# Zeros for the routed rows in two parts, another column order, ranks and slot table earlier in the last step

## What is computed

```
x = x + _layernorm(_L0_attn_ref(_layernorm(x), ...))
xf = _layernorm(x).reshape(-1, C)
shared = geglu(xf, w1s, w2s, w3s)
idx = jnp.argmax(xf @ Wg, axis=-1)
for e in range(N_EXPERTS):
    y = geglu(xf, W1[e], W2[e], W3[e])      # (256, 1024), (256, 1024), (1024, 256)
    final = final + jnp.where((idx == e)[:, None], y, 0.0)
x = x + _layernorm(shared + final)
```

## Time and profile before

| | us |
|---|---|
| median of 3 runs | 1071.74 (1070.04 to 1072.08) |
| the profiled execution's own time | 1071.29 |
| its span in the trace | 1069.4 |
| PE busy in the span | 932.4 (87%) |
| DVE, ACT, POOL busy | 770.1, 599.7, 592.8 |

### The profile page before, as it was taken

The page is one execution under the profiler, slowest core; times in us unless marked ns, Lnnn a source line. Parts: engine busy times, 40 slices in busy tenths (PEclk is TensorE's granted clock), DMA queues, the critical chain, the costliest instruction groups (busy, mean ns, idle before and its releaser), DMA issues.

```text
span 1069.4 us, 28305 instructions
## 1 busy us (share of the span) xinstructions
PE 932.4 (87%) x9798; PEld 830.3 (78%) x9798; DVE 770.1 (72%) x1680; ACT 599.7 (56%) x1031; POOL 592.8 (55%) x802
## 2 busy tenths in 40 slices
PE   2285999999999899899899898845999999999994
PEld 2264787887787787788787787645999999999994
DVE  6889999999999999999999974531444444444443
ACT  5386687688688688678678665312333333333331
POOL 5435477577477577577578523222545455555553
PEclk9687999999999999999999998887999999999998
DMA  6120441441441341341343323298577886585620
GB/s 234 51 89 10 138 159 43 139 159 40 137 157 42 135 157 50 127 157 55 132 147 119 119 80 119 108 371 286 187 236 244 272 275 221 191 262 179 207 66 21
DMA packets 84130, 158.35 MB, mean 148 GB/s; under 512 B 5421, under 2 KB 62894, under 8 KB 78960
## 3 DMA queue, kind: packets, MB, share of 16 engines
q1 hardware_dynamic: 32560, 74.87, 19.9%
q10 hardware_dynamic: 46960, 65.85, 19.0%
q0 software_dynamic: 4560, 16.98, 4.1%
HBM read 178.31 MB, written 52.64 MB: 216 GB/s over the span
## 4 chain that ended last, share of the span: by engine, by line
PE 28%; DVE 26%; issue 14%; POOL 9%; ACTq 5%; ACT 3%; DMA 2%; SPq 2%; DVEq 0%; POOLq 0%
PE up L318 6%; PE up L319 6%; PE up L320 6%; DVE mixed L952 3%; PE yp L320 2%; PE yp L319 2%; PE yp L318 2%; DVE er L1022 2%; ACTq L828 2%; DVE gu L1149 2%; DVE arena L927 2%; POOL inv L1403 2%; DVE val L1037 2%; POOL sh_s L1484 2%; DVE state L1001 2%
## 5 line engine op out<-in xcount | busy, mean ns | idle before, releaser
L318 PE MATMUL up<-mix_s,arena 128*128 128x128 f16 x1248 | 212.1, 220 | 0.9 <-DVE mix_s L1351 0.5
L319 PE MATMUL up<-mix_s,arena 128*128 128x128 f16 x1248 | 212.1, 220 | 0.0
L320 PE MATMUL up<-mix_s,arena 128*128 128x128 f16 x1248 | 212.0, 220 | 0.0
L1484 POOL TENSOR_TENSOR sh_s<-gu,sh_s 128x512 f16<-128x512 f32 x64 | 81.9, 1281 | 169.4 <-ACT sh_s L731 169.3
L318 PE MATMUL up<-xf_s,arena 128*128 128x256 f16 x512 | 142.3, 278 | 0.0
L320 PE MATMUL up<-xf_s,arena 128*128 128x256 f16 x512 | 142.2, 278 | 0.0
L319 PE MATMUL up<-xf_s,arena 128*128 128x256 f16 x512 | 142.2, 278 | 0.0
L1575 POOL TENSOR_TENSOR kf_s<-ex,kf_s 128x512 f16<-128x512 f32 x78 | 90.3, 1157 | 86.2 <-ACT kf_s L889 86.1
L1356 DVE SCALAR_TENSOR_TENSOR ex<-up,ex 128x512 f32<-128x512 f32 x78 | 54.0, 692 | 103.7 <-ACT ex L883 103.6
L318 PEld LDWEIGHTS up<-mix_s,arena 128*128 128x128 f16 x1248 | 122.5, 98 | 2.4 <-DVE ex L1356 1.1
L319 PEld LDWEIGHTS up<-mix_s,arena 128*128 128x128 f16 x1248 | 122.5, 98 | 0.4
(11 more groups left out here) (234 smaller groups left out, 2976.7 us busy)
## 6 DMA issues: line engine op xcount, KB each, us to landing
arena<-w_split ACTq DMA_DIRECT2D x117, 1024.0 KB
arena<-in_W SPq DMA_DIRECT2D x24, 1024.0 KB, 8.1
w_split<-arena SPq DMA_DIRECT2D x24, 1024.0 KB, 8.3
rows<-routed_rows ACTq DMA_DIRECT2D x39, 260.0 KB
routed_rows<-ex SPq DMA_DIRECT2D x8, 1170.0 KB, 12.9
normed<-routed_rows ACTq DMA_DIRECT2D x39, 128.0 KB
x_in<-in_x SPq DMA_DIRECT2D x16, 256.0 KB, 2.8
x_res<-in_x SPq DMA_DIRECT2D x16, 256.0 KB, 2.7
```

The costliest lines, as they stand in the source:

```text
L318: pe.matmul(out, stat(0), mov(0), start=first, stop=False)
L319: pe.matmul(out, stat(0), mov(1), start=False, stop=False)
L320: return pe.matmul(out, stat(1), mov(0), start=False, stop=last)
L1484: pool.tensor_tensor(sh_s[:, 1, 2 * g:2 * g + 2, :], gu[g % GUS][:], sh_s[:, 0, 2 * g:2 * g + 2, :], ALU.subtract).then_inc(S("sh_lo"), 1)
```

## The change

The records' columns are put in another order: the shared part first, then X1, then ID, OFF and XF, so that ID, OFF and XF are one part of 260 floats. The zeros are written in two parts. The first writes columns ID and up only, over five blocks of 128 rows for each expert, at the end of step 15 (when chunk 13 is placed), from a cleared piece of `x_in`; the scatter of chunk 14 waits for it. The second writes the first 520 columns of one block of 128 rows for each expert, in step 17, behind the last placing. In step 17 the ranks, the placing and the slot table are computed next to the gate's choice, woven into the first two shared products; the scatter of the part with XF comes first on POOL; the split of (7, 2) on DVE moves from step 17 to the end of step 16; and ACT loads slot 1's weights after it has copied the shared output (`second_slot`).

```diff
-XF, SHARED, X1, ID, OFF = 0, PART, PART + C, PART + 2 * C, PART + 2 * C + 1
+SHARED, X1, ID, OFF, XF = 0, PART, 2 * PART, 2 * PART + 1, 2 * PART + 4
-        zero_row = ex.rearrange("p n k c -> p (n k c)")[:, 0:ROW]
+        zero_row = x_in.rearrange("p t d -> p (t d)")[:, 0:ROW - ID]
+        zero_rest = ex.rearrange("p n k c -> p (n k c)")[:, 2 * CT * CH:2 * CT * CH + ID]
# SP
-                n = CH // P + 1
+                n = 2 * CH // P + 1
...
-                    sp.dma_start(routed_rows[bass.ds(at, n * P)].rearrange("(n p) d -> p n d", p=P),
-                                 zero_row.unsqueeze(1).broadcast_to([P, n, ROW])).then_inc(S("zeroed"), 16)
+                    sp.dma_start(routed_rows[bass.ds(at, n * P), ID:].rearrange("(n p) d -> p n d", p=P),
+                                 zero_row.unsqueeze(1).broadcast_to([P, n, ROW - ID])).then_inc(S("zeroed"), 16)
+            def zeros_at_ends():
+                sp.wait_ge(S("end_at"), 1)
+                sp.wait_ge(S("zero_rest"), 1)
+                for e in range(E):
+                    at = sp.value_load(end_at[0:1, e:e + 1], min_val=0, max_val=E * REGION - P)
+                    sp.dma_start(routed_rows[bass.ds(at, P), 0:ID], zero_rest).then_inc(S("zeroed_rest"), 16)
...
-                    if at_step(i, NC) and m == 1:
-                        zeros_behind_tokens()
                     store_expert(e, m)
+                if at_step(i, NC - 1):
+                    zeros_behind_tokens()
+                if at_step(i, NC + 1):
+                    zeros_at_ends()
# PE
                 shared_gate(0)
+                if at_step(i, NC + 1):
+                    ranks()
                 shared_gate(1)
...
-                if at_step(i, NC + 1):
-                    ranks()
# ACT
                 if at_step(i, NC + 1):
-                    first_slots()
+                    first_slot()
...
                 y_shared()
                 xf()
+                if at_step(i, NC + 1):
+                    second_slot()
# DVE
                 if at_step(i, NC + 1):
                     gate(c2)
+                    placing(c2, p, h - 1)
+                    dve.wait_ge(S("next_row"), NC)
+                    dve.tensor_copy(end_at[:], next_row[:, 0, :]).then_inc(S("end_at"), 1)
+                    parts()
+                    slots_of_experts()
...
-                early_lo()
+                if not at_step(i, NC + 1):
+                    early_lo(i, p, h)
...
                 shared(0)
+                if at_step(i, NC + 1):
+                    places_of_slots()
                 shared(1)
                 if at_step(i, NC + 1):
-                    placing(c2, p, h - 1)
-                    parts()
+                    last_slots()
...
-                if at_step(i, NC):
+                if at_step(i, NC - 1):
                     zeros_after()
...
+                if at_step(i, NC):
+                    early_lo(NC + 1, 1, h)
+                    dve.wait_ge(S("num"), NC)
+                    dve.wait_ge(S("denominator"), 4 * NC)
+                    dve.memset(zero_rest, 0.0).then_inc(S("zero_rest"), 1)
# POOL
-                        pool.wait_ge(S("zeroed"), 16 * E)
+                def scatter_expert_input():
+                    if at_step(i, NC + 1):
+                        wait(pool, S("xf"), TT * (c2 + 1))
+                        wait(pool, S("off"), c2 + 1)
+                        pool.wait_ge(S("parts"), 1)
+                        scatter_part(2, "scattered_xf")
...
                 now_of()
+                scatter_expert_input()
                 sh_lo(0)
```

More of the change, by code:

```diff
@@ L152, in build @@
         zero_at = sb("zero_at", [E], I32)
+        end_at = sb("end_at", [E], I32)
         ones_row = sb("ones_row", [E])
@@ L163, in build @@
         slot_x = [normed[0][:, 0, :], normed2[:, 0, :]]
-        slot_rest = [rows[b][:, 1, SHARED:] for b in range(2)]
+        slot_rest = [rows[b][:, 1, 0:OFF + 1] for b in range(2)]
         slot_xs = [mix_s[b][:, :, :, 0:P] for b in range(2)]
@@ L852, in load_x, with first_slot @@
                 act.dma_start(slot_x[b], routed_rows[rows_of(n), XF:XF + C]).then_inc(S(f"slot_x_in{b}"), 16)
-            def first_slots():
+            def first_slot():
                 act.wait_ge(S("slot_table"), 2)
@@ L866, in first_slots, with second_slot @@
                     load_x(n, n)
+            def second_slot():
                 for part in range(2):
@@ L1160, in own, with early_lo @@
                         own_lo(n)
-                def early_lo():
+                def early_lo(i, p, h):
                     for e, m in early_piece(i, p, h):
@@ L1233, in step @@
                     x3_sum(c1)
-                if at_step(i, NC + 1):
-                    slots_of_experts()
                 shared(3)
@@ L1251, in step @@
                     next_ids(c1, 1 - p)
-                if at_step(i, NC + 1):
-                    places_of_slots()
-                    last_slots()
+                if at_step(i, NC):
[3 more added lines that the diff above has]
+                    dve.memset(zero_rest, 0.0).then_inc(S("zero_rest"), 1)
                 own(2)
             def zeros_after():
-                dve.wait_ge(S("num"), NC)
-                dve.wait_ge(S("denominator"), 4 * NC)
+                dve.wait_ge(S("normed"), TT * NC)
                 dve.memset(zero_row, 0.0).then_inc(S("zero_row"), 1)
-                dve.wait_ge(S("next_row"), NC - 1)
+                dve.wait_ge(S("next_row"), NC - 2)
                 dve.tensor_copy(zero_at[:], next_row[:, 0, :]).then_inc(S("zero_at"), 1)
@@ L1516, in scatter @@
                 def scatter():
-                    if at_step(i, NC + 1):
-                        wait(pool, S("xf"), TT * (c2 + 1))
-                        pool.wait_ge(S("zeroed"), 16 * E)
[L1521 to L1527, removed]
+                    if on(c2) and not at_step(i, NC + 1):
+                        if at_step(i, NC):
+                            pool.wait_ge(S("zeroed"), 16 * E)
                         wait(pool, S("placed"), c2 + 1)
@@ L1535, in scatter, with scatter_rest @@
                                 in_=rows[p][:, t, :], in_offset=None).then_inc(S(f"scattered{p}"), 16)
+                def scatter_expert_input():
[4 more added lines that the diff above has]
+                        scatter_part(2, "scattered_xf")
+                def scatter_rest():
+                    if at_step(i, NC + 1):
+                        scatter_part(1, "scattered_rest")
+                        pool.wait_ge(S("y_sh"), c2 + 1)
+                        scatter_part(0, "scattered_rest")
                 delta2_of()
@@ L1552, in step @@
                 scatter()
+                scatter_rest()
             chunk_steps(pool, step)
```

4 lines of the change are left out of this document (3 added, 1 removed).

## The result

| | before | changed |
|---|---|---|
| median, us | 1070.89 (1069.77 to 1072.08, 4 runs) | 1054.99 (1054.43 to 1057.17, 4 runs) |
| ratio, 95% interval | | 0.9855, 0.9836 to 0.9874 |
| profiled execution, us | 1071.29 | 1054.43 |
| its span, us | 1069.4 | 1052.3 |

The change takes 15.9 us off the medians. The forecast was 1059.6 us with a range from 1055.5 to 1065: the direction and the place were right, the time lies 0.5 us under the range. (The median of the kernel before was 1071.74 us when the forecast was made; a fourth run of 1069.77 us has moved it to 1070.89.)

A forecast was written before the change was run, and what follows sets the result against it. PE's 23.0 us wait for a transfer behind 9.6 MB of zeros was taken to bound the kernel. A restart at 720.1 instead of 732.17, 12.1 us off 1071.74, gave 1059.6 us, range 1055.5 to 1065.

The forecast's parts named there:

- What bounds the kernel, and the release: Between the phases: PE idles 23.0 us behind zeros and stores; afterwards ACT's last `sh_hi` releases the slots, at 708.5.
- near 7 us: Sign of being right: PE's idle time before the slots' first transposes, ended by the input's transfer.
- The sum: PE restarts at 720.1 instead of 732.17, 12.1 us less, taken off the median of 1071.74: 1059.6 us.
- Step 17, in the old trace's time: Walk through step 17 from the old trace's times: last `sh_hi` ends at 706.4 instead of 704.43, 1.95 us late.
- The delay at POOL: End of step 16: DVE's split of (7, 2) blocks POOL's last product, so step 17 starts 2.1 us later.
- Rival 1: POOL is not blocked, or the table meets no subtraction: restart 2 to 4 us earlier, 1055.5 to 1057.5; 15%.
- The weave: Step 17: ranks, placing and table between the shared products make the last `sh_hi` 1.95 us late, bounds 0.7 to 3.
- From release to PE: Last `sh_hi` to PE's restart: 10.8 us as before, plus 0.8 for the scatter's bytes; from 708.5 to 720.1.
- Rival 2: Slots' start: shared DMA engines or late slot 1 weights cost 3 to 8 us, 1062 to 1068; 15%.
- Eight us of cover, so nothing: Steps 15 and 16: the load of (7, 2) lands at 670 to 672, ACT needs it at 680.01; no cost.
- Rival 3: Slow first zeros make (7, 2) late and delay `expert_hi`; loses from 12.1 us late, 1075 at 135 GB/s; 4%.
- The clock at the restart: PE's granted clock at the slots' start: no gain put down; staying up would give back about 2 us.

The follow-up runs named there:

- before_again: The kernel before, with no edit, run once more on one chip with the changed kernel: 1069.18 us (12 runs).
- after_again: The changed kernel, with no edit, run once more on that chip: 1055.02 us (4 runs), ratio 0.9866 to the kernel before.
- before_p1: The kernel before, with no edit, a single execution on a second chip for its profile: 1069.17 us.

## Why the prediction was right, and where it failed

**What bounds the kernel, and the release: right.** The wait for the stores behind the zeros is gone, the last `sh_hi` releases the slots, the wait left is 5.8 us for the input of slot 0 ("near 7 us"), and the slot phase passes all of it on.

**The sum: 5.0 us short at the restart.** Counted from the placing of step 16 (684.22 before, 681.25 after):

| term | forecast | measured | off |
|---|---|---|---|
| end of step 16 | 684.22 | 681.25 | 2.97 |
| POOL's product behind the split | 2.1 late | 1.67 late | 0.43 |
| last `sh_hi` ends, by the weave | 1.95 late | 1.43 late | 0.52 |
| from there to PE | 11.6 | 10.51 | 1.09 |
| restart | 720.1 | 715.07 | 5.03 |

(The forecast rounded the release up by 0.02.)

- **The step that failed is the base of "Step 17, in the old trace's time"**: I took the times of one execution as those of the program. At the restart this is 2.97 of the 5.03 us. That execution had 7 us at the lower clock in step 16, worth 2.7 to 2.8 us up to the placing, which two of four profiles of the same kernel do not have. The earlier trace rows show the clock for the slots' start alone; I never looked at it in step 16, and so neither the forecast nor the range had a term for it.
- **In the time, the base of the sum failed with it.** The median of three runs, 1071.74, was high: later runs give 1068.7 to 1069.6. The other three terms of the table are 2.0 us, which makes a gain of 14.1 us; the runs of `before_again` and `after_again` show 14.2 to 14.6. From 1071.74 a gain of 14.1 gives 1057.6, inside the range; from the later medians it gives 1054.6 to 1055.5, at or under its end. Whether the low clock is what made the first runs slow is open: from the gate's product to the end the four profiles lie within 1.5 us of each other (418.1 and 417.6 us with it, 416.7 and 417.8 without).
- **The delay at POOL: right in its mechanism, 0.4 us off in size.** The product was blocked for as long as the split still ran. The Trainium skill, "SBUF — State Buffer", section "Who interferes with whom", says that a DVE instruction with two SBUF inputs and a GpSimd instruction that reads SBUF exclude each other; the trace agrees, with 1.87 us for 0.20. Rival 1 named 1055.5 to 1057.5 for the case that POOL is not blocked. The time came close to it, its mechanism did not happen.
- **The weave: right, 0.5 us off.** Both instructions that I expected beside a subtraction met one (1.26 and 1.15 us); the last `sh_hi` lost 1.4 us, not 1.95. The run with the late table shows that the weave is worth about 3 us (2.5 to 2.9 at the restart, 3.5 by the medians).
- **From release to PE: 1.1 us off.** The issue followed the release after 0.43 us, not 1.0, since no transfer's landing ended ACT's wait; and the second zeros had been issued by 700.9, not by 710, so they shared nothing with the weights. From issue to PE it is 10.1 us against 9.8 in the earlier trace rows and 10.04 in `before_p1`: of the 0.8 us that I added for the scatter at most 0.3 shows. Rival 2 did not come.
- **"Eight us of cover, so nothing": wrong, though it cost nothing.** The zeros left at the time forecast (issued 648.5, load of (7, 2) issued 663.2 for "about 662"). But I asked only when the load lands, and not which stores release the buffer that ACT writes. The cover ahead of ACT was under 1 us. Rival 3's mechanism is real, and its point was misplaced in the other direction as well: 5 us of ACT's idle time absorb part of it, so the change loses from about 19 us on, not from 12.1.
- **The clock at the restart: right to give it nothing.** It was 0.50 at 716. Keeping it up brought no time that can be told.

## What to carry to other kernels

A bulk transfer that stands in a queue ahead of small stores is paid by whoever waits for those stores: list every consumer behind it, the stores that free a buffer as well as the loads, both where it leaves and where it goes. When it is moved under other work, take only the columns and rows that the next reader needs. And when a sum is built on one trace, look at the granted clock along the whole stretch first: two of four profiles here lacked the low spell, and the range must hold the execution without it. Then follow the difference to the end of the trace: what a stretch gains is not yet what the run gains.

## What the runs showed of the hardware

- The same program, with the same idle spells of PE around the gate of step 16 (0.81 and 1.46 us both in the first profile of before and in `before_p1`), is granted 0.50 for some 7 us in one execution and 1.00 in another. This is worth 2.7 to 2.8 us at the end of the step; at the end of the four profiles no such difference can be told (418.1 and 417.6 us, 416.7 and 417.8). Taking away a delay of 1.67 us on another engine brought 3.8 us of the medians in one pair of runs and 0.1 to 0.2% against other chips; in the first pair's profiles the rest of it is a low clock in step 17, which came and went without that delay too.
- A DVE instruction of 2.29 us with two SBUF inputs stretches even the issue of an indirect transfer on POOL, from 1.04 to 2.59 us.
- Writes in pieces of 1040 B from SBUF to HBM ran at 346 GB/s with the DMA engines full, for 12.4 us of issues.
